# A two-layer block with two attentions: the head norms of the second attention spread over three quarters of a batch, reciprocal roots by one third-order and one Newton step

## Time and profile before

| | us |
|---|---|
| median of 3 runs (lowest to highest) | 2566.45 (2564.83 to 2569.43) |
| span of the profiled execution | 2561.3 |
| PE / DVE / ACT / POOL busy | 2081.4 / 1929.2 / 1471.9 / 1215.3 |

### The profile page before, as it was taken

One profiled execution on the slowest core, in us unless ns is written; L12 is line 12 of the kernel. 1 busy time (PEld: TensorE's weight loads), 2 busy tenths in 40 slices (PEclk: granted clock), 3 DMA queues, 4 the chain that ended last, 5 costly groups with the idle time before them and its releaser, 6 DMA issues. The chain is left out here.

```text
span 2561.3 us, 47512 instructions
## 1 busy us (share of the span) xinstructions
PE 2081.4 (81%) x14760; PEld 1019.2 (40%) x14760; DVE 1929.2 (75%) x5688; ACT 1471.9 (57%) x3368; POOL 1215.3 (47%) x1708
## 2 busy tenths in 40 slices
PE   1799999999987884898989898964667988898692
PEld 0222222222222553444444444433445666675471
DVE  7599999999994873777787778847776676776364
ACT  0388888888885221566666666742334555555251
POOL 0534343434310003566667666524444777652776
PEclk9999999999999996799999999976888999999796
DMA  3433333232313902323232323211222433332353
GB/s 83 99 76 76 76 76 77 67 85 62 90 27 139 386 2 50 93 60 90 62 91 62 90 63 90 63 51 56 71 72 80 126 112 112 111 108 78 104 149 100
DMA packets 226244, 228.14 MB, mean 89 GB/s; under 512 B 33360, under 2 KB 189136, under 8 KB 226000
## 3 DMA queue, kind: packets, MB, share of 16 engines
q1 hardware_dynamic: 153056, 165.73, 24.2%
q0 software_dynamic: 16384, 33.59, 4.5%
q10 hardware_dynamic: 56560, 25.78, 3.5%
HBM read 97.07 MB, written 126.35 MB: 87 GB/s over the span
## 5 line engine op out<-in xcount | busy, mean ns | idle before, releaser
L618 ACT ACTIVATE l_PT<-l_ps 128x512 f32<-128x512 f32 (+2 forms) x1792 | 915.6, 568 | 313.1 <-PE l_ps L502 305.2
L698 DVE TENSOR_REDUCE l_nmax<-l_ps 128x1 f32<-128x512 f32 (+2 forms) x1280 | 777.7, 657 | 91.7 <-PE l_ps L483 62.9
L483 PE MATMUL l_ps<-KT,QT 48*128 48x512 bf16 (+3 forms) x2048 | 612.3, 354 | 104.7 <-DVE l_nmax L698 48.6
L502 PE MATMUL l_ps<-QT,KT 64*128 64x512 bf16 (+3 forms) x2048 | 567.2, 349 | 3.0 <-ACT l_PT L618 2.6
L518 PE MATMUL l_ps<-l_PT,vv 128*32 128x512 f32 (+3 forms) x4096 | 472.7, 535 | 15.4 <-POOL l_PT L814 11.1
L1150 PE MATMUL moe_ps<-moe_w,moe_xinT 128*128 x656 | 359.2, 631 | 88.4 <-DVE moe_h L1312 88.0
L483 PEld LDWEIGHTS l_ps<-KT,QT 48*128 48x128 bf16 x2048 | 160.3, 94 | 630.9 <-DVE l_nmax L698 400.3
L695 DVE CUSTOM_DVE_ANT_0 l_thrown<-l_ps,mask 128x512 bf16<-128x512 f32 (+1 forms) x512 | 305.2, 619 | 111.8 <-PE l_ps L483 108.5
L1263 POOL DMA_INDIRECT rows_in<-moe_xn,moe_scat_idx x256 | 247.2, 966 | 265.5 <-DVE moe_scat_idx L1450 188.5
L1207 ACT ACTIVATE moe_xinT<-moe_ps,norm_w 128x128 f32<-128x128 f32 x328 | 120.1, 366 | 356.4 <-PE moe_ps L1164 349.7
L1276 POOL DMA_INDIRECT moe_yg<-rows_out,moe_gat_idx x256 | 245.4, 958 | 78.0 <-issue 76.8
(11 more groups left out here) (241 smaller groups left out, 3221.2 us busy)
## 6 DMA issues: line engine op xcount, KB each, us to landing
l_spread<-l_slots SPq DMA_DIRECT2D x128, 384.0 KB, 5.1
rows_in<-ffn_blank SPq DMA_DIRECT2D x4, 8192.0 KB, 48.2
QT<-l_spread SPq DMA_DIRECT2D x128, 192.0 KB, 4.4
KT<-l_spread SPq DMA_DIRECT2D x128, 192.0 KB, 5.2
moe_xin<-rows_in SPq DMA_DIRECT2D x328, 64.0 KB
rows_out<-moe_y ACTq DMA_DIRECT2D x328, 64.0 KB
x<-in_L_attn_x_dram SPq DMA_DIRECT2D x8, 512.0 KB, 7.2
QT<-l_mrows SPq DMA_DIRECT2D x256, 6.0 KB
```

What stands on the lines that cost most here:

```text
L483: mm = pe.matmul(ps[:, bank, n_keys * a:n_keys * (a + 1)], QT[rows, par, pair, i * P:(i + 1) * P], KT[rows, par, pair, 0:n_keys], start=Tr ...
L502: mm = pe.matmul(ps[:, bank, m * a:m * (a + 1)], KT[rows, own, pair, i * P:(i + 1) * P], QT[rows, own, pair, SEQ - m:SEQ], start=True, sto ...
L618: act.activation(weights_of(r, i, heads), ps[:, ring(S2, n - 2, k), 0:widths[i] * len(heads)], ACT.Exp, scale=scale).then_inc(exp_done, 1)
L698: dve.tensor_reduce(to, of, X_AXIS, ALU.max, negate=True).then_inc(s1_used, 1)
```

## The change

The three Newton steps become one third-order step and one Newton step. The third-order step is four operations (`cubic_root`: square, times v; `cubic_step`: t (t - 10/3), then y (t + 5)); it leaves the value scaled, and `newton` carries the factor 0.375 in its constants. A root has eight operations instead of ten, everywhere.

In the second attention the pieces also move: `variance(0)` from quarter 2, u=0 to quarter 1, u=9; `variance(1)` from u=2 to u=1; scale and seed from u=3 to u=4; the first half of the third-order step at u=8 of quarter 2; its second half at u=0 of quarter 3 and the Newton step at u=3 of quarter 3. On POOL the multiplication by the roots goes behind the addition of the projection.

```diff
-RSQRT_LINKS = 9
+SEED_LINKS, CUBIC_LINKS, NEWTON_LINKS = 1, 4, 2
+RSQRT_LINKS = SEED_LINKS + CUBIC_LINKS + NEWTON_LINKS
+CUBIC = 0.375
...
+def cubic_root(c, y, v, t):
+    c.link(c.eng.tensor_tensor(t, y, y, ALU.mult))
+    c.link(c.eng.tensor_tensor(t, v, t, ALU.mult))
+
+def cubic_step(c, y, t):
+    c.link(c.eng.scalar_tensor_tensor(t, t, -10.0 / 3.0, t, ALU.add, ALU.mult))
+    c.link(c.eng.scalar_tensor_tensor(y, t, 5.0, y, ALU.add, ALU.mult))
 
 def newton(c, y, v, t):
     e = c.eng
     c.link(e.tensor_tensor(t, y, y, ALU.mult))
-    c.link(e.scalar_tensor_tensor(t, v, -0.5, t, ALU.mult, ALU.mult))
-    return e.scalar_tensor_tensor(y, t, 1.5, y, ALU.add, ALU.mult)
+    c.link(e.scalar_tensor_tensor(t, v, -0.5 * CUBIC ** 3, t, ALU.mult, ALU.mult))
+    return e.scalar_tensor_tensor(y, t, 1.5 * CUBIC, y, ALU.add, ALU.mult)
 
 def rsqrt(c, y, v, t):
     rsqrt_seed(c, y, v)
-    for k in range(2):
-        c.link(newton(c, y, v, t))
+    cubic_root(c, y, v, t)
+    cubic_step(c, y, t)
     return newton(c, y, v, t)
...
-                    if causal and qd == 2 and within(b + 2, BATCHES):
+                    if causal and qd in (1, 2, 3) and within(b + 2, BATCHES):
                         head = Chain(dve, head_chain, HEAD_LINKS * (b + 2))
-                        if u == 0:
+                        var_, root, scratch = gvar[:, :], grs[:, :], gtmp[:, :]
+                        if qd == 1 and u == 9:
                             dve.wait_ge(squared, 2 * (b + 2) + 1)
                             variance(0)
-                        if u == 2:
+                        if qd == 2 and u == 1:
                             dve.wait_ge(squared, 2 * (b + 2) + 2)
                             head.link(variance(1))
-                        if u == 3:
+                        if qd == 2 and u == 4:
                             head.n = 1
-                            head.link(dve.tensor_scalar(gvar[:, :], gvar[:, :], 1.0 / HD, 1e-5, ALU.mult, ALU.add))
-                            rsqrt_seed(head, grs[:, :], gvar[:, :])
-                        if u in (5, 7):
-                            head.n = 3 * ((u - 3) // 2)
-                            head.link(newton(head, grs[:, :], gvar[:, :], gtmp[:, :]))
-                        if u == 9:
-                            head.n = 9
-                            newton(head, grs[:, :], gvar[:, :], gtmp[:, :]).then_inc(rstd_ready, 1)
+                            head.link(dve.tensor_scalar(var_, var_, 1.0 / HD, 1e-5, ALU.mult, ALU.add))
+                            rsqrt_seed(head, root, var_)
+                        if qd == 2 and u == 8:
+                            head.n = 2 + SEED_LINKS
+                            cubic_root(head, root, var_, scratch)
+                        if qd == 3 and u == 0:
+                            head.n = 4 + SEED_LINKS
+                            cubic_step(head, root, scratch)
+                        if qd == 3 and u == 3:
+                            head.n = 2 + SEED_LINKS + CUBIC_LINKS
+                            newton(head, root, var_, scratch).then_inc(rstd_ready, 1)
...
-                if causal and qd == 3 and within(b + 2, BATCHES):
-                    pool.wait_ge(rstd_ready, b + 3)
-                    for a in range(2):
-                        view = qk[:, a, :].rearrange("p (g e c) -> p g e c", e=HD, c=8)
-                        by = grs[:, 64 * a:64 * a + 64]...
-                        done = pool.tensor_tensor(view, view, by, ALU.mult)
-                    done.then_inc(qk_ready, 1)
...
                     pool.wait_ge(g_used, 2 * (b - 2) + 2)
                     xs = x[:, bass.ds(4 * (b - 2), TILES), :]
                     pool.tensor_tensor(xs, xs, proj[:, :, :], ALU.add).then_inc(x_added, 1)
+                if causal and qd == 3 and within(b + 2, BATCHES):
+                    pool.wait_ge(rstd_ready, b + 3)
+                    ... (the six lines above, unchanged)
```

More of the change, by code:

```diff
@@ L775, in step @@
                     pool.tensor_tensor(xn[:, :, :], xn[:, :, :], rstd, ALU.mult).then_inc(xn_ready, 1)
-                if causal and qd == 3 and within(b + 2, BATCHES):
-                    pool.wait_ge(rstd_ready, b + 3)
-                    for a in range(2):
-                        view = qk[:, a, :].rearrange("p (g e c) -> p g e c", e=HD, c=8)
-                        by = grs[:, 64 * a:64 * a + 64].rearrange("p (g c) -> p g c", c=8).unsqueeze(2).to_broadcast([P, 8, HD, 8])
-                        done = pool.tensor_tensor(view, view, by, ALU.mult)
-                    done.then_inc(qk_ready, 1)
                 def split(a):
@@ L809, in step @@
                     pool.tensor_tensor(xs, xs, proj[:, :, :], ALU.add).then_inc(x_added, 1)
+                if causal and qd == 3 and within(b + 2, BATCHES):
+                    pool.wait_ge(rstd_ready, b + 3)
+                    for a in range(2):
+                        view = qk[:, a, :].rearrange("p (g e c) -> p g e c", e=HD, c=8)
+                        by = grs[:, 64 * a:64 * a + 64].rearrange("p (g c) -> p g c", c=8).unsqueeze(2).to_broadcast([P, 8, HD, 8])
+                        done = pool.tensor_tensor(view, view, by, ALU.mult)
+                    done.then_inc(qk_ready, 1)
                 if causal and within(n - 2, STEPS):
@@ L1381, in side @@
                         rsqrt_seed(c, rstd[:, :], m2[:, :])
-                        c.link(newton(c, rstd[:, :], m2[:, :], tmp[:, :]))
+                        cubic_root(c, rstd[:, :], m2[:, :], tmp[:, :])
                     if s == 3:
-                        c.link(newton(c, rstd[:, :], m2[:, :], tmp[:, :]))
+                        cubic_step(c, rstd[:, :], tmp[:, :])
                         c.link(newton(c, rstd[:, :], m2[:, :], tmp[:, :]))
@@ L1400, in side @@
                     rsqrt_seed(c, rstd[:, :], var[:, :])
-                    c.link(newton(c, rstd[:, :], var[:, :], tmp[:, :]))
-                if s in (7, 8):
+                    cubic_root(c, rstd[:, :], var[:, :], tmp[:, :])
+                if s == 7:
+                    cubic_step(c, rstd[:, :], tmp[:, :])
+                if s == 8:
                     c.link(newton(c, rstd[:, :], var[:, :], tmp[:, :]))
```

## The result

The changed kernel takes 2497.83 us (median of 4 runs, 2495.88 to 2501.23) against 2566.01 us for the kernel before (4 runs): ratio 0.9733, 95% interval 0.972 to 0.9747. That is 68.2 us less; 62 were forecast (2504, range 2489 to 2528). The profiled execution took 2495.88 us with a span of 2494.1 us. So what lies around a span is 1.8 us there, not the 5.15 that I took; the difference of two medians doesn't depend on it.

What follows compares the result with a forecast made beforehand. DVE was taken to bound quarter 2 of second attention, with a clock bill in quarter 3. Gains of 50.4 (attention), 6.0 (feed-forward), 1.0 (centers), 0.65 (attention's start) and 4.0 (experts) sum to 62.05: 2566.45 to 2504 us, range 2489 to 2528.

Steps and rivals of the forecast that it cites:

- Quarter 2 is DVE's: Second attention: DVE, busy 12.69 of 13.07 us, sets quarter 2 and only that one.
- The slot walk: Second attention, quarters 2 and 3 walked slot by slot: 18.6 us against 22.46, 3.9 a batch.
- The price of the head norms' work: Second attention: head norms' DVE work with its consequences costs 4.67 us a batch, judged against batch 14 without them.
- The size of the attention's gain: Second attention: 3.6 us a batch after leaving 0.3 for jitter, 50.4 us in 14 batches.
- the clock's bill: Second attention: PE's wait in quarter 2 lowers its clock soon after; V projection takes 1.94 us instead of 1.13.
- Quarter 1 at nothing: Second attention: the variance adds 1.04 us to DVE in quarter 1, hidden by waits and slack, costed at nothing.
- The swap on POOL at nothing: Second attention, quarter 3: multiplication by the roots still fits ahead of the corner operations, about 0.5 us to spare; no cost.
- The shorter root: Outside the attention's batches: feed-forward 6.0 us, centers 1.0, second attention's start 0.65, experts 4.0 (between 3.2 and 9.6).
- The whole cost goes: Rival, second attention: quarters 2 and 3 come near batch 14's, gaining about 4.4 us a batch, 61.6; total 2493; 15%.
- The moved work lands on the path: Rival, quarter 3: the five moved operations delay PE's transpose, only 2.05 us a batch stays; total 2526; 18%.
- The moved operations meet POOL: Rival, quarter 3: one DVE operation a batch waits out POOL's 1.28 us addition, 18 us come back; total 2522; 9%.
- Slower, by the clock: Rival, second attention: a further quarter of each batch at 1.2 GHz, 6 us more a batch, 84; total 2588; 4%.

Runs made afterwards that it cites:

- no_head_roots: Changed kernel without the head norms' variances and roots in batches 2 to 15, one memset of a constant in their place; 2488.72 us, ratio to before 0.9699.
- cubic_in_place: Changed kernel's shorter root everywhere, but head norms' variances and root operations at their old units in quarter 2 and POOL's old order; 2538.61 us, ratio to before 0.988.
- newton_late: Changed kernel with the Newton step of quarter 3 at unit 8 instead of unit 3; 2534.34 us, ratio to before 0.9873.
- xn_early: Changed kernel with POOL's normalization of x moved from quarter 0 to quarter 2 of the batch before, in second attention; 2488.97 us, ratio to before 0.9692.
- variance_moved: Shorter root everywhere, first variance at quarter 1, unit 9, all head-norm root operations still in quarter 2, POOL's old order; 2534.47 us, ratio to before 0.9866.
- pad1: Changed kernel plus one needless variance (1.04 us) on DVE in quarter 2, unit 6, of 14 batches; 2525.03 us, ratio to before 0.9824.
- pad3: Changed kernel plus three needless variances (3.1 us in one piece) on DVE in quarter 2, unit 6; 2564.24 us, ratio to before 0.9987.
- variance_back: Changed kernel with the first variance back in quarter 2, unit 0; 2513.29 us, ratio to before 0.9797.
- newtons_spread: Changed kernel with the old root of three Newton steps in the head norms alone, at the spread places; 2503.71 us, ratio to before 0.9749.
- pool_order_before: Changed kernel with POOL's multiplication by the roots ahead of the addition of the projection again; 2508.53 us, ratio to before 0.9776.
- experts_old_root: Changed kernel with the old root of three Newton steps in the experts only; 2501.78 us, ratio to before 0.9741.

## Why the prediction was right

**Quarter 2 is DVE's.** Right, for the kernel before; in the changed one DVE and the rest are even there, as the prediction said (nearly) they would be. The slot walk gave 9.4 + 9.2 = 18.6 us for quarters 2 and 3; measured are 9.57 + 9.09 = 18.66. The price of the head norms' work, 4.67 us a batch, or 65 in 14, came near (68 by no_head_roots), but with some luck: the pair of quarters it started from was about 0.3 short of the mean, and batch 14's 17.79 about as much below the 18.09 that the pair takes in no_head_roots from batch 2 on.

**The size of the attention's gain.** 50.4 us forecast, 56.6 measured, 4.04 a batch over 14 batches instead of 3.6 (4.14 over batches 1 to 13). Two parts were off. I took the pair of quarters in the earlier trace rows as typical, 22.46 us; the mean pair of before is 22.81, since in every other batch the clock stayed low longer:

```profile
1334.44:1347.09 12.65, 9.47 (x96) 4.57 (x95) 12.27 (x35) 6.55 (x14) 3.42 (x9) 1.00 0.77 197
1347.09:1357.48 10.39, 9.83 (x94) 4.48 (x93) 7.33 (x24) 7.08 (x17) 6.96 (x11) 0.84 0.03 8
```

These are quarters 2 and 3 of the next batch of before: shorter, then longer, 23.04 in all. And the 0.3 us a batch left for jitter was not needed: 18.6 was met within 0.1.

**Why it gained.** The prediction priced the moves by DVE's durations and named the clock's bill without a term of its own. Most of the gain is where it put it: of the 4.14 us a batch, 3.31 lie in quarter 2, where DVE's back-to-back work became shorter (3.68 forecast), and 0.84 in quarter 3. The clock's part can be read against the 8.82 us that quarter 3 takes in cubic_in_place at clock 1.00: before, it took 1.11 more in the mean; in the changed kernel it takes 0.27 more, at clock 1.00, with five root operations in it. In the steps between, the clock weighs more. Without batches 14 and 15, shortening the root alone took 16 us off the attention; moving the variance as well, 7 more; and the rest of the change (half of the root into quarter 3, the other pieces one or more units later, POOL's order) 34 more, for 1.63 us a batch of DVE work that leaves quarter 2. 1.63 x 14 is 23. The rest came when PE's late gap went and with it the slow stretch: quarter 3 fell from 10.26 to 9.09 although 1.6 us of DVE work were added to it. The order of the steps matters for such shares (the variance is worth 7 us with the slow stretch still there, 13 without it), so no single number belongs to each part.

**Quarter 1 at nothing.** Right: 9.39 in the kernels that have the variance there, as in those that have not. The two exceptions, newton_late and xn_early with 9.83, are those in which quarter 1's first mark comes earlier behind the last maximum (0.85 us instead of 1.7).

**The swap on POOL at nothing.** Right as the changed kernel stands, with the 0.5 us to spare that I gave it; without the swap it would have cost 8 to 11 us.

**The shorter root.** The feed-forward's 0.40 a batch is there to a hundredth (1.06 to 0.67), but not in all 16 batches: from its first to its last transpose the stage is 4.9 us shorter (812.65 to 955.23 before, 812.91 to 950.58 now), since the first two batches are no shorter (the third transpose had waited 0.29 us before and waits for nothing now); 6.0 were forecast. Up to the first mark 7.65 were forecast (6.0, 1.0 and 0.65) and 5.8 measured; kernels with the same setup, first attention and feed-forward lie between 1018.6 and 1020.5, so this is 5.3 to 7.2. The experts' 4.0 is unresolved. Inside the attention, my removal of 0.65 a batch counts in full only while all the work sits in quarter 2; in the spread place it is worth 0.1. So the sum of 62 against 68.2 measured is an attention term 6.2 too small and a term up to the first mark some 2 too large; for the experts' term the profiles give 4.7, but their scatter is larger.

**The rivals.** None came true. *The whole cost goes*: 61.6 forecast, 56.6 measured; the remaining 11 us lie in quarter 3 (0.57 a batch) more than in quarter 2 (0.15). *The moved work lands on the path*: about 0.3 us a batch of its 1.63 does (9.09 against the 8.82 at full clock without it), and what the full clock gives back is more. *The moved operations meet POOL*: no operation was stretched; the addition ended 0.18 us ahead of the Newton step, so the order of the operations keeps the two apart. That the stretch of L83 in before, which came in 12 batches, is the exclusion that the Trainium skill describes ("SBUF — State Buffer", section "Who interferes with whom") fits these rows, but it isn't shown: no run put a two-input operation beside a long POOL operation and another operation in its place. And beside POOL's short operations the overlap costs next to nothing. In the changed kernel L91 runs from 1310.52 to 1310.81, in its usual 0.29 us, and POOL's L784 starts at 1310.63, inside that time, and takes 0.25 instead of the 0.22 us of L785 behind it. *Slower, by the clock*: not in the changed kernel, but variance_moved, pad1 and pad3 show that the clock can fall with the work spread otherwise, at 1.4 to 1.8 us a batch in the mean (up to 2.9 in one batch of cubic_in_place). The prediction let it decide from two thirds of a quarter a batch on; 62 of 84 us is nearer three quarters.

## What to carry to other kernels

When one engine's extra work makes a long quarter in a regular pipeline, compare with a period in which that work is missing (here the last batches): it gives the price with all its consequences, and a floor. Such a floor may be a little low: quarter 2 of batch 14 was 0.3 us below that of the middle batches of no_head_roots. Spread such work so that the engine it holds up has no long gap late in the quarter; PE's clock bill, where it comes, arrives one quarter later, in rows where nothing seems wrong. Look at every period, not at one: the same program paid that bill in half of them. And check first whether the operation count is worth reducing once the work is spread: here it was some 2 us in the attention, against 54 for the places (657.5 to 603.9, with the old root).

## What was not expected of the hardware

The same 1.04 us of DVE work in the same quarter lengthened the attention (without batches 14 and 15) by 13.4 us at its start and by 30.7 us in its middle. PE had a gap of 0.99 us in the first case, early, and the clock stayed at 1.00 in batches 1 to 13; in the second the gaps were 0.80 and 0.27 us, late, in front of the next quarter, and the granted clock of the next quarter was 0.88. With the gap of 1.00 us late, in variance_moved, it was 0.88 too. Before fell to 0.84 or 0.95 by turns from batch to batch with nearly the same program around it. So the size of a gap alone does not tell what it costs. Nor does the sum of the gaps: PE was busy 9.15 of 10.60 us in that quarter of variance_back and 9.08 of 10.15 in that of pad1, so it stood idle longer where the clock stayed.

The place of the gap in the quarter doesn't settle it either. In cubic_in_place the gap of 0.99 us stands 9 us into quarter 2 in each of batches 2 to 13, and the clock fell behind six of them and not behind the other six. Nor is there need of a difference ahead of it. These are the last two quarters of batch 15 in the changed kernel and in newtons_spread, with the same program; the first of each pair is alike in every engine, and the clock of the second is 1.00 or 0.83:

```profile
1602.69:1612.24 9.55, 8.66 (x94) 4.07 (x92) 7.53 (x22) 6.46 (x15) 3.24 (x10) 1.00 0.01 2
1612.24:1620.78 8.54, 7.27 (x83) 3.25 (x83) 6.88 (x23) 6.32 (x15) 4.51 (x10) 1.00 0.01 3
...
1604.63:1614.18 9.55, 8.67 (x94) 4.07 (x92) 7.53 (x22) 6.45 (x15) 3.24 (x9) 1.00 0.01 2
1614.18:1624.08 9.90, 8.63 (x83) 3.34 (x83) 6.95 (x23) 6.41 (x15) 4.51 (x10) 0.83 0.01 3
```

So something that isn't in the kernel's own order of work must count too, perhaps the moment at which the gap falls. No run varied that alone, and it is open whether pad1's clock falls in every batch for the place of its gap or for the length of its batch. What the profiles do show is that in the kernels whose quarter 2 has, from batch 2 on, no gap above 0.46 us in its second half (the changed one, newtons_spread, variance_back, pool_order_before, no_head_roots, xn_early, experts_old_root) the clock of quarters 2 and 3 was 1.00 in all of batches 1 to 13.
